# Decoder block on one core: first FFN split, last value spread, tail and first step reordered

## What is computed

```python
def attn(x):                     # 16 heads of 64
    Q, K, V = x@W_Q + b_Q, x@W_K + b_K, x@W_V + b_V
    a = softmax(Q @ K.T / 8)
    return sum_over_heads(a @ V @ W_O) + b_O
def xattn(q, c):                 # the 16 heads of ONE token attend to each other
    q, k, v = q@Wq.T + bq, c@Wk.T + bk, c@Wv.T + bv
    a = softmax(einsum("bshd,bsgd->bshg", q, k) / 8)
    o = einsum("bshg,bsgd->bshd", a, v)
    return o.transpose(0, 2, 1, 3).reshape(b, -1, 1024) @ Wo.T + bo
def ffn(x):                      # 128 of 128 tokens are routed: every token takes both paths
    n = x / norm(x) * sqrt(128)
    return gelu(n*g_l @ W1_l + b) @ W2_l + b + gelu(n*g_h @ W1_h + b) @ W2_h + b
x = layernorm(x + attn(x)); x = layernorm(x + xattn(x, ctx)); x = layernorm(x + ffn(x))
```

## Time and profile before

| | us |
|---|---|
| median of three runs | 413.41 (412.16 to 416.49) |
| profiled execution | 414.85 |
| its span, first to last instruction | 413.0 |
| TensorE busy in the span | 398.8 |
| VectorE busy | 287.6 |
| ScalarE busy | 240.1 |
| POOL busy | 148.1 |

### The profile page before, as it was taken

How to read it: one execution, slowest core, us unless ns; L and a number is a source line. 1 busy time by engine, 2 the same in 40 slices (tenths; PEclk the granted TensorE clock), 3 DMA queues, 4 the chain that set the end, 5 groups by cost and what they waited for, 6 DMA issues and landing times.

```text
span 413.0 us, 15941 instructions
## 1 busy us (share of the span) xinstructions
PE 398.8 (97%) x6580; PEld 344.6 (83%) x6580; DVE 287.6 (70%) x661; ACT 240.1 (58%) x813; POOL 148.1 (36%) x224
## 2 busy tenths in 40 slices
PE   8999999999999999999999999999999999798996
PEld 7787888788888888888888898888989888687884
DVE  4686786866848678667757868659566967578445
ACT  5675574745567466655566566457466648336351
POOL 0642434432413454323315444213324445123213
PEclk9999999999999999999999999999999999899999
DMA  7900113110110213100201112200201121102001
GB/s 262 356 5 8 44 26 83 46 32 9 33 23 19 45 32 87 41 14 8 42 13 32 37 41 75 51 2 17 44 8 39 27 49 22 33 12 43 27 26 52
DMA packets 43646, 19.27 MB, mean 47 GB/s; under 512 B 36592, under 2 KB 40944, under 8 KB 43584
## 3 DMA queue, kind: packets, MB, share of 16 engines
q1 hardware_dynamic: 42736, 16.88, 15.8%
q0 software_dynamic: 560, 1.38, 1.0%
q10 hardware_dynamic: 288, 0.07, 0.1%
HBM read 8.88 MB, written 1.05 MB: 24 GB/s over the span
## 4 chain that ended last, share of the span: by engine, by line
PE 83%; DVE 6%; ACT 4%; SPq 3%; issue 2%; DMA 1%; POOL 1%; POOLq 0%; DVEq 0%
PE ps L1151 8%; PE ps L1206 7%; PE ps L1139 7%; PE ps L1063 7%; PE ps L1118 6%; PE ps L1127 6%; PE ps L1035 6%; PE ps L1015 5%; PE ps L1017 4%; PE ps L1016 4%; PE ps L1161 4%; PE ps L1054 3%; SPq L309 3%; PE ps L1145 2%; ACT p L535 2%; PE ps L1094 2%
## 5 line engine op out<-in xcount | busy, mean ns | idle before, releaser
L535 ACT ACTIVATE p<-ps,neg_max 128x128 f32<-128x128 f32 x256 | 90.0, 383 | 42.9 <-DVE neg_max L799 42.9
L406 POOL TENSOR_TENSOR p<-p,row_inv 128x1024 f32<-128x1024 f32 x32 | 60.7, 1896 | 61.7 <-DVE row_inv L805 61.7
L528 ACT ACTIVATE pt<-ps 128x512 f32<-128x512 f32 x62 | 34.5, 625 | 48.7 <-PE ps L1118 48.7
L535 ACT ACTIVATION_READ_ACCUMULATOR p<-ps,neg_max 128x1 f32 x256 | 57.6, 225 | 0.0
L799 DVE TENSOR_REDUCE neg_max<-ps 128x4 f32<-128x512 f32 x64 | 41.5, 671 | 5.6 <-PE ps L1206 4.8
L745 DVE TENSOR_TENSOR ot<-ps,bv 128x512 f32<-128x512 f32 x32 | 22.0, 688 | 30.7 <-PE ps L1139 30.5
L1118 PE MATMUL ps<-ident,p 128*128 128x128 f32 x256 | 34.8, 279 | 1.3 <-POOL p L406 1.3
L1127 PE MATMUL ps<-x1t,wq 128*64 128x64 f32 x1024 | 34.0, 224 | 1.9 <-issue 1.0
L1206 PE MATMUL ps<-kt,qt 64*64 64x128 f32 x1024 | 35.1, 275 | 0.0
L1127 PEld LDWEIGHTS ps<-x1t,wq 128*64 128x64 f32 x1024 | 31.5, 138 | 3.5 <-issue 2.4
L1139 PEld LDWEIGHTS ps<-pt,v 128*64 128x64 f32 x512 | 28.9, 141 | 6.1 <-issue 6.1
(11 more groups left out here) (153 smaller groups left out, 838.1 us busy)
## 6 DMA issues: line engine op xcount, KB each, us to landing
v<-v2s SPq DMA_DIRECT2D x256, 32.0 KB
xg<-x_t SPq DMA_DIRECT2D x4, 256.0 KB, 3.0
pt<-w_qk SPq DMA_DIRECT2D x4, 256.0 KB, 5.1
cg<-ctx_t SPq DMA_DIRECT2D x4, 256.0 KB, 3.6
wo<-w_o SPq DMA_DIRECT2D x2, 512.0 KB, 9.2
xres<-x_nat SPq DMA_DIRECT2D x15, 64.0 KB, 1.7
out<-x2b SPq DMA_DIRECT2D x3, 256.0 KB, 2.3
p<-w_v SPq DMA_DIRECT2D x1, 512.0 KB, 7.0
```

The lines of the kernel that those rows point to most:

```text
L406: nc.gpsimd.tensor_tensor(ph, ph, row_inv[:, 8 * half:8 * half + 8].unsqueeze(2).to_broadcast([T, 8, T]), ALU.mult).then_inc(p_ready, 1)
L528: nc.scalar.activation(pt[:, u * BANK:(u + 1) * BANK], bank(T_BANK[u]), ACT.Copy).then_inc(pt_ready, 1)
L535: last = nc.scalar.activation(p[:, hd * T:(hd + 1) * T], bank(S_BANK[q])[:, pos * T:(pos + 1) * T], ACT.Exp, bias=neg_max[:, hd:hd + 1], a ...
```

## The change

Five edits, in one kernel:
1. `f_high(0)` and `f_low(0)` move from behind step 15 into it: on ACT between the third and the last group of exponentials, on DVE between the second write of `v2s` and the copies of the queries.
2. The last spread (batch 15) goes to `v[0]`, a buffer of self-attention values that is free by then. SP waits for the `weighted` of step 15 instead of `weighted_v2(16)`; `weighted_v2(17)` reads `v[0]`.
3. On DVE `y_out(0)` moves behind the two `block_diagonal` of batch 15.
4. At the end the scaling of a batch comes after the sums of the two batches behind it, where it came after one.
5. The start. ACT, not SP, issues the first quarter of `wqk`. The first unit's three matmuls wait one by one for what each needs. `wv` is loaded into a part of `x2b` that is free, its split comes behind block D, and in step 0 PE does scores, all eight `k2` units, values, transposes, in this order.

```diff
+        v2_last = v[0]
-        wqk, wv, wv2 = pt, p, v2
+        wqk, wv, wv2 = pt, x2b, v2
...
-            for u in range(4):
+            for u in range(1, 4):
                 sp.dma_start(wqk[:, u * BANK:(u + 1) * BANK], w_qk[:, u * BANK:(u + 1) * BANK]).then_inc(in_wqk[u], 16)
...
-            def spread_values2(s, d):
-                if d:
+            def spread_values2(s, d, dst=v2):
+                if dst is not v2:
+                    sp.wait_ge(mm_pv, 2 * B - 2)
+                elif d:
                     sp.wait_ge(mm_pv2, 2 * s - 2)
                 sp.wait_ge(v2s_ready, 2 * s)
...
-            spread_values2(B, True)
+            spread_values2(B, True, v2_last)
...
+            act.dma_start(wqk[:, 0:BANK], w_qk[:, 0:BANK]).then_inc(in_wqk[0], 16)
             act.dma_start(bqk[:], b_qk).then_inc(in_bqk, 16)
...
+                if phase == 0 and a:
+                    qk_out(g, "D")
                 if static and s == 0:
                     split_hi(4)
                     split_hi(5)
-                if phase == 0 and a:
-                    qk_out(g, "D")
...
+                if static and s == B - 1:
+                    f_high(0)
                 if d:
                     regrouped(s)
...
                     split_hi(6)
                     split_hi(7)
+                    values_out(0, 0)
...
-            f_high(0)
...
-                if static and s == 0:
-                    split_lo(4)
-                    split_lo(5)
...
                     score_max(3)
+                    split_lo(4)
+                    split_lo(5)
...
+                if static and s == B - 1:
+                    f_low(0)
...
-            f_low(0)
...
-            y_out(0)
             block_diagonal(LAST, 0)
             block_diagonal(LAST, 1)
+            y_out(0)
...
-                if bb:
-                    scale3_of_batch(bb - 1)
+                if bb > 1:
+                    scale3_of_batch(bb - 2)
+            scale3_of_batch(GB - 2)
             scale3_of_batch(GB - 1)
...
+                    pe.wait_ge(x_hi, 1)
+                    pe.wait_ge(w_hi, WQK_SPLIT[0])
+                    nc.tensor.matmul(bank(FIRST_BANKS[0]), wqk_hi[:, 0:128], xg_hi[:], start=True, stop=False)
                     pe.wait_ge(x_lo, 1)
+                    nc.tensor.matmul(bank(FIRST_BANKS[0]), wqk_hi[:, 0:128], xg_lo[:], start=False, stop=False)
                     pe.wait_ge(w_lo, WQK_SPLIT[0])
-                    project_qk(0, "A", lambda r: None, FIRST_BANKS)
+                    nc.tensor.matmul(bank(FIRST_BANKS[0]), wqk_lo[:, 0:128], xg_hi[:], start=False, stop=True).then_inc(mm_qk, 1)
+                    project_qk(0, "A", lambda r: None, FIRST_BANKS, units=(1, 2, 3))
...
+                if static and s == 0:
+                    read(1, (0, "C"))
+                    read(3, (0, "C"))
+                    scores(0)
...
+                    read(1, (0, "D"))
+                    read(3, (0, "D"))
                 if a:
                     scores(1)
...
-                    project_k2(0, "E", lambda r: read(r, (0, "D")), units=(1, 2, 3))
+                    pe.wait_ge(in_wk2, 16)
+                    pe.wait_ge(in_cg, 16)
+                    project_k2(0, "E", lambda r: None)
                     project_k2(0, "F", lambda r: read_k2(r, "E"))
+                    pe.wait_ge(exp_ready, 2)
+                    pe.wait_ge(w_lo, WV_SPLIT)
+                    values(0)
                     pe.wait_ge(in_ident, 16)
+                    pe.wait_ge(v_ready, 2)
...
-            weighted_v2(LAST, 0)
-            weighted_v2(LAST, 1)
+            weighted_v2(LAST, 0, v2_last)
+            weighted_v2(LAST, 1, v2_last)
```

More of the change, by code:

```diff
@@ L308, in spread_values2 @@
                             col = ((pp * J + j) * IH + ih) * DH
-                            sp.dma_start(v2[:, col:col + DH],
+                            sp.dma_start(dst[:, col:col + DH],
                                          v2s[first:first + (K - 1) * 2 * J + 1:2 * J, :].rearrange("k (g d) -> k g d", g=H)
@@ L537, in exponentials, with values_out @@
                     last.then_inc(exp_ready, 1)
+                def values_out(s, par):
+                    for u in range(2):
+                        act.wait_ge(mm_v, 2 * s + u + 1)
+                        nc.scalar.activation(v[par][:, u * BANK:(u + 1) * BANK], bank(V_BANK[u]), ACT.Copy).then_inc(v_ready, 1)
                 static = isinstance(s, int)
@@ L563, in step @@
                     split_hi(5)
-                if phase == 0 and a:
-                    qk_out(g, "D")
                 if phase == 1 and a and not static:
                     k2_out(g, "F")
[L568 to L571, removed]
+                if a and bc:
+                    values_out(s, par)
                 if d and not projecting:
@@ L1043, in transpose_p2, with weighted_v2 @@
                 last.then_inc(mm_pt2, 1)
-            def weighted_v2(s, ih):
+            def weighted_v2(s, ih, src=v2):
                 pe.wait_ge(pb_ready, 2 * (s - 2) + 2)
@@ L1054, in weighted_v2 @@
                         last = nc.tensor.matmul(bank(PV2[k2])[64 * pp:64 * pp + 64, e * 64:(e + 1) * 64],
-                                                v2[rows, (q * IH + ih) * DH:(q * IH + ih + 1) * DH],
+                                                src[rows, (q * IH + ih) * DH:(q * IH + ih + 1) * DH],
                                                 pb[rows, (ih * 2 * J + q) * 64:(ih * 2 * J + q + 1) * 64], start=True, stop=True)
@@ L1141, in weighted, with values @@
                     last.then_inc(mm_pv, 1)
+            def values(phase):
+                own = slice(phase * T, (phase + 1) * T)
+                for u in range(2):
+                    cols = slice(u * BANK, (u + 1) * BANK)
+                    nc.tensor.matmul(bank(V_BANK[u]), xg_lo[:, own], wv_hi[:, cols], start=True, stop=False)
+                    nc.tensor.matmul(bank(V_BANK[u]), xg_hi[:, own], wv_hi[:, cols], start=False, stop=False)
+                    nc.tensor.matmul(bank(V_BANK[u]), xg_hi[:, own], wv_lo[:, cols], start=False, stop=True).then_inc(mm_v, 1)
             def values2(u, own):
@@ L1234, in step @@
                     project_k2(g, "F", lambda r: read_k2(r, "E"))
-                if a:
-                    if static and s == 0:
-                        pe.wait_ge(w_lo, WV_SPLIT)
-                    if bc:
-                        pe.wait_ge(pt_ready, 4 * s - 4 + 2)
-                    own = slice(phase * T, (phase + 1) * T)
-                    for u in range(2):
-                        cols = slice(u * BANK, (u + 1) * BANK)
-                        nc.tensor.matmul(bank(V_BANK[u]), xg_lo[:, own], wv_hi[:, cols], start=True, stop=False)
-                        nc.tensor.matmul(bank(V_BANK[u]), xg_hi[:, own], wv_hi[:, cols], start=False, stop=False)
-                        nc.tensor.matmul(bank(V_BANK[u]), xg_hi[:, own], wv_lo[:, cols], start=False, stop=True).then_inc(mm_v, 1)
+                if a and bc:
+                    pe.wait_ge(pt_ready, 4 * s - 4 + 2)
+                    values(phase)
                 if bc:
                     weighted(s, b_par)
-                if a:
+                if static and s == 0:
+                    read(1, (0, "C"))
+                    read(3, (0, "C"))
+                    scores(0)
+                elif a:
                     if phase == 0:
@@ L1253, in step @@
                         read(3, (g, "D"))
-                    if s == 0:
-                        pe.wait_ge(in_wk2, 16)
-                        pe.wait_ge(in_cg, 16)
-                        project_k2(0, "E", lambda r: read(r, (0, "D")), units=(0,))
                     pe.wait_ge(v_ready, 2 * s + 2)
```

## The result

The changed kernel takes 410.31 us, the median of 10 runs (409.95 to 411.34); the kernel before takes 414.01 in the same comparison (10 runs, 412.16 to 416.49). The ratio is 0.9918 with an interval of [0.9891, 0.9944]: faster by 0.8%. The interval leaves out 1, so the gain is real, and it reaches both sides of the 1% at which the prediction drew its line. The profiled execution takes 410.04 us with a span of 408.2; before it took 414.85 with a span of 413.0, so 4.81 less.

The account below looks back on a forecast made before the run. TensorE, busy 97% of the span, was taken as the bound, so only its idle or slow stretches counted. 2.3 + 1.6 + 1.05 + 0 + 0.2 = 5.15 us off 413.41 gave 408.3, range 406.8 to 411.0.

Parts of the forecast that it names:

- rival 1: Tail: the low clock appears all the same, or the timed runs mostly lacked it; 409.9 us, chance 0.18.
- the 0.68: Whole kernel: the predicted chance of measuring faster, below the line of 409.3 us; slower had 0.03.
- The idle, 2.3 us: Step 15: with the split moved in, TensorE no longer waits for `xg_lo` before the first FFN product; 2.3 us removed.
- The slow clock, 1.6 us: Tail, behind that idle: the low clock goes with the idle; 1.6 us won, bounds 0 and 1.7.
- the 5.15: Whole kernel: the predicted total gain in us, 2.3 + 1.6 + 1.05 + 0 + 0.2.
- The last values, 1.05 us: Tail: spread into `v0` and swap let TensorE start at 380.3 to 380.4 instead of 381.40; 0.9 without the swap.
- rival 2: Tail: the stall at 381.40 is only replaced, by `block_diagonal` or `xn`, and the first step gives nothing; 409.2 us, chance 0.14.
- The scalings, 0: End: sums ahead of scalings change only when earlier batches are scaled; 0 taken, 0 to 0.3 us lost by crowded stores.
- The first step, +0.2 us: Start: quarter issued by ScalarE and the new order of step 0 win 0.2 us; bounds -0.6 and +0.5.
- g: Start: gain at the third matmul, taken as 0.3 us; at most 0.46, or -0.1 if the two loads interleave.
- Rival 3: Start: bias `bqk` lands late behind ScalarE's quarter, delaying the second matmul and bringing the low clock, 1.6 us; slower, chance 0.03.
- g less 0.1: Rest of step 0: the new order passes on about g less 0.1, so 0.2 us, to the second transposes.

## Why the prediction was right, and where not

The direction and the place were right: three terms of the sum, all in the tail, carry the gain. Two steps of the reasoning failed: the sign of the term for the first step, and the step from the profiled execution to the median. So 410.31 lies inside the range, but near its upper end and nearer to rival 1's 409.9 than to the 408.3, and what came was the outcome within 1%, which had 0.29, not the 0.68. (The upper end's own terms, 413.41 - 2.3 - 1.05 + 0.6, give 410.7, not 411.0.)

- **The idle, 2.3 us.** Right, 2.53 in the traces. I had costed the two instructions ahead of `q2_out` at nothing, with POOL's second scaling ending near 351.9; it ended at 350.03 + 1.90 = 351.93. I had the regrouping of step 15 later by 0.7 us, but followed it to POOL only: TensorE reads it too, and waited 0.63 us for it at 349.48. That this cost nearly nothing between the two traces I had no reason to expect: in its place a pause by "issue" of 0.53 us at 347.86 was gone, so that the transposes came only 0.32 later, 0.06 more than step 15's `weighted`.

- **The slow clock, 1.6 us.** The size is right, 1.57 between the profiles: from the first up product to the first `wv` product behind `weighted` it is 3.48 us (353.37 to 356.85) where it was 5.05. That the clock falls whenever the idle is there was not so: the spread alone shows the idle of 2.29 us and no drop. The Trainium skill, TensorE: Matmul & The Clock Gate (Part 1, The HAM clock gate), says of a kernel's start that the same kernel measures different numbers of slow matmuls from run to run. These runs show the like in mid-kernel: a mean clock of 0.995 or less in 13 of 25 executions where the idle stands, and in none of 12 where it is filled.

- **From one execution to the median.** This is the step that cost most. I wrote "The three runs have a median 1.44 lower, 413.41; less 5.15 that is 408.3". The 1.6 us in the 5.15 was read from an execution that had the drop, and a good part of the median's executions has none to lose. My first rival held this in its second half, "the timed runs mostly lacked it", at 0.18; of the ten runs of before in this comparison, five lie at 412.16 to 413.41 and five at 414.61 to 416.49. That the 413.41 of three runs became 414.01 with ten is a further 0.6 us of the miss. Against the profiled execution of before, the sum gave 409.7 and the profiled one of after measured 410.04. The measured gain is 414.01 - 410.31 = 3.70, so 1.45 of the 5.15 are missing. Against the upper five alone (median 414.70) the gain is 4.39, so by an estimate 0.7 of the 1.45 is the drop that half of the executions did not have. The first step was to give 0.2 and gave about nothing. The other half microsecond is not placed, and the share of executions with the drop is not behind it, since a gap is there in each group alone: beside the kernel with edits 1 to 4 alone (410.46), the 13 runs of before at the low mean clock have a median of 414.53 and the other 12 one of 412.7. That is a gain of 4.1 and of 2.2, where the sum without the first step has 4.95 and 3.35. Shown of this is one part: where the clock had not fallen (the idle filled), the wait for the spread was 0.7 us, not 1.1, so there was less of it to remove:

```profile
PE ps L1054 <- DMA v<-v2s: 0.7, 1, 0.7
```

  The rest stays open. The trace of before has two pauses by "issue", 0.44 and 0.53 us, that the changed kernel's has not; other traces of either kernel have shorter ones or longer, so the 4.81 between these two traces can be more than what the medians gain.

- **The last values, 1.05 us.** 1.03 in the traces. The buffer was free as I read it, and `weighted_v2` waits for nothing. The swap was mis-sized: I took 0.1 to 0.2 us ("Without the swap, 0.9"), and without it the wait for `pt` is 0.4 in both traces that lack it, so some 0.6 is nearer. That wait is the mechanism of rival 2, but only where the swap is left out, and at half the size that rival needed.

- **The scalings, 0.** Right: 1.77 us from the last sum to the last scaling with either order.

- **The first step, +0.2 us.** Wrong in sign. The failed step is "I take 0.3" for g, the gain at the third matmul. `xg` landed 1.06 us later with a second load issued at the same time (3.81 to 4.87). The Trainium skill, DMA: Bandwidth & Descriptors (Issuing engines are not separate DMA queues), says that loads started by different engines run on the same DMA engines and interleave with each other. The trace agrees. With the quarter issued 0.45 us later, though (the bias first), `xg` was not late at all and the quarter was, so the rule alone doesn't say which of two loads pays. I had it in the text with g = -0.1 and went by the other value. Rival 3's late bias came too: the bias was there near 6.0 us where I estimated 4.5, far from the 8.8 at which it would have decided. The second matmul stood where that rival's L + 1.0 puts it (6.97), but the low clock that it added did not come: the granted clock from 6 to 8 us is 1.00. Together the third matmul stood at 7.57 and not 6.37, so g was -0.9 by the prediction's own 6.67, and -0.82 by the 6.75 of the timeline. The second half, "g less 0.1", held within 0.2: `weighted` of step 1 is 0.82 later. The sign that I gave for it, the second transposes near 30.1, missed by a microsecond (30.22 is the first half, the second stands near 31.1). The size, though, is partly luck of the trace that I went by, the earliest of five with the old first step; between the means it is 0.5. What I had not foreseen is that this loss hardly reaches the end: between the two traces 0.56 us of it comes back, and the kernel with the old first step measures the same (410.46). The order of step 0 is not at its best either: with the quarter on SP and the values between the `k2` blocks, 408.80 was measured.

## What to carry to other kernels

A low clock behind an idle of TensorE need not be there in every execution: before its price is taken off a median, look at whether the runs fall into groups, by time and by mean granted clock, and size the term by the share that has it; filling the idle with dummy products prices the clock alone. A load issued from a second engine to bring one operand forward can delay what was first before (here by 1.06 us) and what stands behind it in its own queue (the bias, there at 6.02 us); ask which of the inputs is needed last. Read a start from more than one trace before a term of half a microsecond is taken from it. A gain at the start of a long loop should be followed to the last step before it is counted.

## What the runs showed of the hardware that I had not expected

TensorE's program, unlike those of the other engines, has no loop: all its steps are written out in full. It stops in two places without a wait that the profile shows. The traces' rows of it, before and with the spread alone:

```profile
197.15 0.81 PE L1127 MATMUL ps<-x1t,wq 128*64 128x64 f32 x21 [0.44 <-issue]
...
347.86 0.51 PE L1127 MATMUL ps<-x1t,wq 128*64 128x64 f32 x10 [0.53 <-issue]
```

```profile
197.78 0.81 PE L1131 MATMUL ps<-x1t,wq 128*64 128x64 f32 x21 [1.03 <-issue]
```

In the five traces with the old first step the pause near 197 us is there, 0.21 to 1.03 us, always ahead of the last 21 matmuls of that group. In the seven with a new first step it is not; four of them have one near 347 us (0.15 to 0.41), and one has 0.18 near 169. These twelve traces show that it goes away with the reordered first step; why is not shown. The loading of TensorE's instructions is an obvious candidate (the page of the profile counts 52 packets on a queue for instructions), and no run tested it.

The second surprise is how much one landing at the start varies. The first weight quarter, 256 KB and issued by SP, was there at 4.70 us before, and at 4.90 to 5.67 in the six other traces that issue it so. It was there at 6.00 when ScalarE issued it second. The start of a single trace is thus known to about a microsecond, more than the first step's term, and the prediction's 4.70 was the earliest of the seven.
